# Threshold search of a graph stage: two staggered groups of tiles, the interval arithmetic and the scaling of x on GpSimd

## The reference, cut to what matters

```python
def _L1_xattn_ref(h, adj_raw, Wq, Wk, gamma_raw):
    ...
    sim = jnp.einsum('bhnd,bhmd->bnm', Q, K) / (jnp.sqrt(jnp.float32(d)) * H)
    k = max(1, int(n * TOP_K_RATIO))                      # 153 of 512
    topk_vals = jax.lax.top_k(sim, k)[0]
    threshold = topk_vals[:, :, -1:]
    sparse_mask = (sim >= threshold).astype(sim.dtype)
    A_learned = jax.nn.sigmoid(sim) * sparse_mask
    A_learned = (A_learned + jnp.swapaxes(A_learned, -1, -2)) * 0.5
    gamma = jax.nn.sigmoid(gamma_raw)
    return (1.0 - gamma) * adj_raw + gamma * A_learned
...
x = _layernorm(x + _L1_xattn_ref(ctx_512, x, ...), axis=-1)
```

## Time and profile before

| | us |
|---|---|
| median of 3 runs | 2637.19 |
| fastest and slowest of them | 2636.38, 2638.69 |
| the profiled execution | 2622.37 |
| its span, first to last instruction | 2620.70 |
| from the stage's first DMA issue to the next stage's first instruction | 1939.74 to 2129.29: 189.6 |
| the search, from DVE's first `mid` to the first mask | 1949.76 to 2066.28: 116.5 |
| masks and layer norm, to the next stage | 2066.28 to 2129.29: 63.0 |

### The profile page before, as it was taken

One profiled execution on the slowest core, in us unless ns is written; L12 is line 12 of the kernel. 1 busy time (PEld: TensorE's weight loads), 2 busy tenths in 40 slices (PEclk: granted clock), 3 DMA queues, 4 the chain that ended last, 5 costly groups with the idle time before them and its releaser, 6 DMA issues. The chain is left out here.

```text
span 2620.7 us, 32973 instructions
## 1 busy us (share of the span) xinstructions
PE 2007.4 (77%) x12156; PEld 1348.8 (51%) x12156; DVE 1763.1 (67%) x2779; ACT 1255.1 (48%) x2238; POOL 719.4 (27%) x662
## 2 busy tenths in 40 slices
PE   5999999377878787789986599999930159979990
PEld 4778777222222222355553477777720138857770
DVE  3456565366768675789997444656648867379986
ACT  2323232157656556367777232323228641169881
POOL 1111212200685950111210211121210002355535
PEclk8899999668889889899997689999965569989995
DMA  5332321356343420400000423232210030099976
GB/s 153 81 74 55 68 57 42 134 122 196 87 141 92 140 54 7 183 1 1 1 1 1 121 49 74 49 74 49 50 64 0 0 116 1 1 391 423 411 283 192
DMA packets 84584, 264.55 MB, mean 101 GB/s; under 512 B 17504, under 2 KB 19040, under 8 KB 73424
## 3 DMA queue, kind: packets, MB, share of 16 engines
q0 software_dynamic: 29632, 151.50, 17.3%
q1 hardware_dynamic: 53776, 110.75, 14.9%
q10 hardware_dynamic: 1024, 0.26, 0.0%
HBM read 169.87 MB, written 41.72 MB: 81 GB/s over the span
## 5 line engine op out<-in xcount | busy, mean ns | idle before, releaser
L880 DVE TENSOR_REDUCE x_negm<-x_M 128x2 f32<-128x1024 f32 x256 | 309.6, 1224 | 110.8 <-PE x_M L940 110.4
L829 ACT ACTIVATE x_PT<-x_T 128x512 f32<-128x512 f32 x512 | 280.2, 598 | 196.0 <-PE x_T L960 190.6
L322 ACT ACTIVATE L_attn_PT<-L_attn_T 128x512 f32<-128x512 f32 x320 | 175.3, 595 | 359.6 <-PE L_attn_T L524 359.6
L392 DVE TENSOR_REDUCE L_attn_negm<-L_attn_M 128x2 f32<-128x1024 f32 (+1 forms) x192 | 192.0, 1041 | 57.3 <-PE L_attn_M L505 56.9
L229 POOL DMA_DIRECT2D L_attn_QKS<-L_attn_HL x64 | 34.8, 544 | 597.3 <-ACT L_attn_HL L307 563.5
L960 PE MATMUL x_T<-x_QS,x_KS 49*128 49x512 f32 x512 | 139.4, 541 | 64.5 <-ACT x_PT L829 43.7
L522 PE MATMUL L_attn_T<-L_attn_QKS 97*128 97x256 f32 (+3 forms) x512 | 164.9, 384 | 10.0 <-DMA L_attn_QKS<-L_attn_mT 7.7
L969 PE MATMUL x_O<-x_PT,x_V 128*32 128x512 f32 x1024 | 155.7, 684 | 8.0 <-issue 8.0
L960 PEld LDWEIGHTS x_T<-x_QS,x_KS 49*128 49x128 f32 x512 | 51.5, 198 | 212.0 <-ACT x_PT L829 134.9
L940 PE MATMUL x_M<-x_KS,x_QS 48*128 48x512 f32 x512 | 119.1, 462 | 43.9 <-DMA x_QS<-x_xl 23.5
L503 PE MATMUL L_attn_M<-L_attn_QKS 96*128 96x384 f32 (+2 forms) x384 | 135.6, 422 | 19.2 <-DVE L_attn_XTL L366 11.5
(11 more groups left out here) (385 smaller groups left out, 5500.3 us busy)
## 6 DMA issues: line engine op xcount, KB each, us to landing
L_attn_QKS<-L_attn_HL SPq DMA_DIRECT2D x192, 128.0 KB, 4.7
L_attn_QKS<-L_attn_HL POOLq DMA_DIRECT2D x192, 128.0 KB, 4.1
moe_y_rows<-slots_YS SPq DMA_DIRECT2D x47, 256.0 KB, 7.0
x_WRAW<-in_w_gateT POOLq DMA_DIRECT2D x8, 1024.0 KB, 7.4
x_QS<-x_xh SPq DMA_DIRECT2D x128, 64.0 KB, 2.4
x_WRAW<-in_w_upT POOLq DMA_DIRECT2D x8, 1024.0 KB, 5.3
x_WRAW<-in_w_downT POOLq DMA_DIRECT2D x8, 1024.0 KB, 6.1
ffn_w<-x_WTER POOLq DMA_DIRECT2D x12, 512.0 KB, 3.0
```

The lines of the kernel that those rows point to most:

```text
L322: ac.activation(PT[:, s, bank], T[:, bank], ACT.Exp, scale=SCALE).then_inc(t_free, 1)
L392: last = ve.tensor_reduce(negm[:, g % 2, h0:h0 + nh, i], src, AX.X, ALU.max, negate=True)
L829: ac.activation(PT[:, s // 4, head(s), :], T[(STEPS_S * g + s) % 3][:], ACT.Exp, scale=SCALE).then_inc(t_free, 1)
L880: ve.tensor_reduce(negm[:, g % 2, u // 4:4:2, u % 4], m[:].rearrange("p (r k) -> p r k", r=2), AX.X, ALU.max, negate=True).then_inc(m_free, 1)
```

## The change

The search is written out (no hardware loop) and its tiles form two groups. Group 0 is tiles 0 to 3 (DVE) and 8 to 11 (ACT), group 1 is tiles 4 to 7 and 12 to 15; `side(col, g)` picks the eight columns of a group as 2 x 4. DVE and ACT count group 0, then group 1, then group 0 of the next halving, each when POOL has raised `mid_made` for it. POOL does the interval arithmetic of a group when both engines have counted it, in six steps of which each waits for the one before. After each halving POOL multiplies one tile of x by g2 in place; `XS` and ACT's 16 scalings are gone, and line 1626 (now 1635) reads x instead of `XS`. `graw` is loaded before the similarities, `gamma` is made before the search, and g2 and gh between DVE's first and second halving.

```diff
@@ block.sync @@
+            sp.dma_start(graw[:], A["gamma"]).then_inc(q["loaded"], 16)
             for b in (0, 2, 1, 3):
                 sp.dma_start(SIM[...], GR["sim"][b]).then_inc(sim_in[b], 16)
-            sp.dma_start(graw[:], A["gamma"]).then_inc(q["loaded"], 16)
+
+        @block.gpsimd
+        def _(pool):
+            PER = 6
+            for g in range(2):
+                gp.tensor_tensor(side(mid, g), side(low, g), side(width, g), ALU.add).then_inc(q["mid_made"], 1)
+            for n in range(HALVINGS):
+                for g in range(2):
+                    step = Steps(pool, q["halving"], 2 * n + g, PER)
+                    pool.wait_ge(q["counted_v"], 2 * n + g + 1)
+                    step(gp.tensor_scalar(side(take, g)[:, 0], side(count, g)[:, 0], TOPK - 0.5, None, ALU.is_ge))
+                    pool.wait_ge(q["counted_a"], 2 * n + g + 1)
+                    step(gp.tensor_scalar(side(take, g)[:, 1], side(count, g)[:, 1], S + 1.5 - 2 * TOPK, None, ALU.is_le))
+                    step(gp.tensor_tensor(side(take, g), side(take, g), side(width, g), ALU.mult))
+                    step(gp.tensor_tensor(side(low, g), side(low, g), side(take, g), ALU.add))
+                    step(gp.tensor_scalar(side(width, g), side(width, g), 0.5, None, ALU.mult))
+                    step(gp.tensor_tensor(side(mid, g), side(low, g), side(width, g), ALU.add))
+                    pool.sem_inc(q["mid_made"], 1)
+                if n == 0:
+                    pool.wait_ge(q["gam2"], 2)
+                gp.tensor_scalar(XF[:, n, :], XF[:, n, :], g2[:, 0:1], 1.0, ALU.mult, ALU.mult).then_inc(q["scaled"], 1)
@@ block.scalar @@
+            act.wait_ge(q["loaded"], 16)
+            ac.activation(gamma[:], graw[:], ACT.Sigmoid).then_inc(q["gam"], 1)
             for b in range(DVE_TILES // NT, NB):
                 act.wait_ge(sim_in[b], 16)
-            with act.Fori(0, HALVINGS) as n:
-                act.wait_ge(q["mid_done"], n + 1)
-                for t in range(DVE_TILES, NTILE):
-
-                    inst = ac.activation(seen_a[:, t - DVE_TILES, :], SIM[:, t, :], ACT.Sign, scale=-1.0,
-                                         bias=mid[:, t:t + 1], accum_out=count[:, t:t + 1])
-                inst.then_inc(q["counted_a"], 1)
-            act.wait_ge(q["loaded"], 16)
-            ac.activation(gamma[:], graw[:], ACT.Sigmoid).then_inc(q["gam"], 1)
+            for n in range(HALVINGS):
+                for h in range(2):
+                    act.wait_ge(q["mid_made"], 2 * n + h + 1)
+                    for t in range(DVE_TILES + HALF * h, DVE_TILES + HALF * (h + 1)):
+                        inst = ac.activation(...)
+                    inst.then_inc(q["counted_a"], 1)
...
-            act.wait_ge(q["gam2"], 2)
...
-                if b:
-                    act.wait_ge(q["z_done"], b * NT)
-                for i in range(NT):
-                    ac.activation(XS[:, i, :], XF[:, b * NT + i, :], ACT.Identity, scale=g2[:, 0:1]).then_inc(q["xs"], 1)
@@ block.vector @@
-            with dve.Fori(0, HALVINGS) as n:
-                k = Steps(dve, q["halved"], n, 4)
-                ve.tensor_tensor(mid[:], low[:], width[:], ALU.add).then_inc(q["mid_done"], 1)
-                dve.wait_ge(q["mid_done"], n + 1)
-                for t in range(DVE_TILES):
...
-                k(ve.scalar_tensor_tensor(out=take[:, 0:DVE_TILES], ...))
-                dve.wait_ge(q["counted_a"], n + 1)
-                k(ve.scalar_tensor_tensor(out=take[:, DVE_TILES:], ...))
-                k(ve.tensor_tensor(low[:], low[:], take[:], ALU.add))
-                k(ve.tensor_scalar(width[:], width[:], 0.5, None, ALU.mult))
+            for n in range(HALVINGS):
+                for h in range(2):
+                    dve.wait_ge(q["mid_made"], 2 * n + h + 1)
+                    for t in range(HALF * h, HALF * (h + 1)):
+                        inst = ve.tensor_scalar(...)
+                    inst.then_inc(q["counted_v"], 1)
+                if n == 0:
+                    dve.wait_ge(q["gam"], 1)
+                    pre = Steps(dve, q["gam2"], 0, 2)
...
+            dve.wait_ge(q["mid_made"], 2 * HALVINGS + 2)
...
-                        dve.wait_ge(q["xs"], b * NT + i + 1)
+                        dve.wait_ge(q["scaled"], b * NT + i + 1)
                         ve.scalar_tensor_tensor(out=XF[:, b * NT + i, :], in0=SUM[:, i, :], scalar=gh[:, 0:1],
-                                                in1=XS[:, i, :], op0=ALU.mult, op1=ALU.add).then_inc(q["z_done"], 1)
+                                                in1=XF[:, b * NT + i, :], op0=ALU.mult, op1=ALU.add).then_inc(q["z_done"], 1)
```

More of the change, by code:

```diff
@@ L1495, in stage_graph @@
         SUM = sb("SUM", [P, NT, S], F32)
-        XS = sb("XS", [P, NT, S], F32)
         seen_v = sb("seen_v", [P, DVE_TILES, S], BF16)
         seen_a = sb("seen_a", [P, NTILE - DVE_TILES, S], BF16)
+        HALF = DVE_TILES // 2
+        side = lambda col, g: col[:].rearrange("p (e t) -> p e t", e=2)[:, :, HALF * g:HALF * (g + 1)]
         graw, gamma, g2, gh = (small(n, 1) for n in ("graw", "gamma", "g2", "gh"))
@@ L1505, in stage_graph @@
         PP = [ps(f"P{i}", 2 * BANK) for i in range(4)]
-        names = ("loaded mid_done counted_v counted_a gam gam2 "
-                 "sigm xs masked turned summed halved z_done stat norm shifted applied between")
+        names = ("loaded mid_made counted_v counted_a halving scaled gam gam2 "
+                 "sigm masked turned summed z_done stat norm shifted applied between")
         sim_in = [sem(f"sim_in{b}") for b in range(NB)]
@@ L1533, in _ @@
         def _(act):
+            act.wait_ge(q["loaded"], 16)
+            ac.activation(gamma[:], graw[:], ACT.Sigmoid).then_inc(q["gam"], 1)
             for b in range(DVE_TILES // NT, NB):
                 act.wait_ge(sim_in[b], 16)
-            with act.Fori(0, HALVINGS) as n:
-                act.wait_ge(q["mid_done"], n + 1)
-                for t in range(DVE_TILES, NTILE):
-                    inst = ac.activation(seen_a[:, t - DVE_TILES, :], SIM[:, t, :], ACT.Sign, scale=-1.0,
-                                         bias=mid[:, t:t + 1], accum_out=count[:, t:t + 1])
-                inst.then_inc(q["counted_a"], 1)
-            act.wait_ge(q["loaded"], 16)
-            ac.activation(gamma[:], graw[:], ACT.Sigmoid).then_inc(q["gam"], 1)
+            for n in range(HALVINGS):
+                for h in range(2):
+                    act.wait_ge(q["mid_made"], 2 * n + h + 1)
+                    for t in range(DVE_TILES + HALF * h, DVE_TILES + HALF * (h + 1)):
+                        inst = ac.activation(seen_a[:, t - DVE_TILES, :], SIM[:, t, :], ACT.Sign, scale=-1.0,
+                                             bias=mid[:, t:t + 1], accum_out=count[:, t:t + 1])
+                    inst.then_inc(q["counted_a"], 1)
             for b in range(DVE_TILES // NT):
                 act.wait_ge(sim_in[b], 16)
-            act.wait_ge(q["gam2"], 2)
             def norm_tile(t):
@@ L1591, in _ @@
-            dve.wait_ge(q["gam"], 1)
-            pre = Steps(dve, q["gam2"], 0, 2)
-            pre(ve.tensor_scalar(g2[:], gamma[:], -1.0, 2.0, ALU.mult, ALU.add))
-            pre(ve.tensor_scalar(gh[:], gamma[:], 0.5, None, ALU.mult))
+            for n in range(HALVINGS):
+                for h in range(2):
+                    dve.wait_ge(q["mid_made"], 2 * n + h + 1)
+                    for t in range(HALF * h, HALF * (h + 1)):
+                        inst = ve.tensor_scalar(seen_v[:, t, :], SIM[:, t, :], mid[:, t:t + 1], 0.0, ALU.is_ge, ALU.add,
+                                                accum_out=count[:, t:t + 1])
+                    inst.then_inc(q["counted_v"], 1)
+                if n == 0:
+                    dve.wait_ge(q["gam"], 1)
+                    pre = Steps(dve, q["gam2"], 0, 2)
+                    pre(ve.tensor_scalar(g2[:], gamma[:], -1.0, 2.0, ALU.mult, ALU.add))
+                    pre(ve.tensor_scalar(gh[:], gamma[:], 0.5, None, ALU.mult))
```

10 lines of the change are left out of this document (removed).

## The result

| | median us | runs | lowest to highest |
|---|---|---|---|
| kernel before, measured beside it | 2639.44 | 9 | 2636.38 to 2650.58 |
| changed kernel | 2626.00 | 9 | 2612.05 to 2635.34 |

What follows compares the result with a forecast made beforehand. The bound was taken to be ACT's counting with DVE's small arithmetic bare behind it in each search halving. Terms summed to -20.3 us, from 2637.2 to 2616.9 us; the range was 2614.5 to 2626.0.

Steps and rivals of the forecast that it cites:

- This chain is the bound: Search: ACT's eight counts, then DVE's small arithmetic lying bare for 1.29 us, make the halving's period of 7.04 us.
- counting, with the borders: Search: ACT's counts take 90.6 instead of 111.30 us, -20.7; 31 new group borders on ACT add 0.6.
- end of the search: From ACT's last count to the first mask: 2.77 us before, POOL's chain of 1.77 after, -1.0.
- last scaling against the first masks: POOL's sixteenth scaling beside DVE's first mask: each can hold the other up, 0 to 0.69 us, taken as +0.3.
- start: Start of the graph stage: SP issues `graw` ahead of the similarities, shifting everything by +0.5 us (0 to 0.6).
- XS gone: Masks: 16 activations of 0.71 us leave ACT, which waited for DVE there; gain 0.
- rival C: Search: group borders on ACT cost 0.21 us each, +5.9, kernel at 2622.8 us; chance 0.07.
- B: POOL's scaling is a slow form, 2.07 us, making POOL the bound; kernel at 2623.1 us; chance 0.22.
- D: Search: POOL is stretched by DVE's counting, 0.8 us more than ACT per halving; kernel at 2628.9 us; chance 0.07.
- E: Search: each POOL step waits for a whole DVE count, 47.4 us over the forecast, 2664.3; chance 0.05.
- It lay 14.8 below the median of the runs, so I carry the difference over: Whole kernel: the profiled execution's 2602.1 us after the change is raised to a median of 2616.9.
- F: Outside the search: something gives the gain back, so no gain; chance 0.04.

Runs made afterwards that it cites:

- a_nostag: Changed kernel without the stagger: both groups wait for the second `mid`; ratio to the kernel before 1.0019, graph stage 194.2 us.
- a_xs: Changed kernel with the scaling of x back on ACT in the masks, none on POOL; ratio to the kernel before 0.9898, graph stage 167.7 us.
- a_slow: Changed kernel with POOL's scaling written as subtract 0, then multiply by g2; ratio to the kernel before 0.9963, graph stage 172.2 us.

## Why the prediction was right, and where it was off

**The bound and the cover: right.** "This chain is the bound" and "ACT never waits for a `mid`" held in every halving; `a_nostag` shows that without the cover nothing of the gain is left. Term by term:

| term | predicted | measured |
|---|---|---|
| counting, with the borders | -20.7 + 0.6 | -20.96 |
| end of the search | -1.0 | -1.13 |
| last scaling against the first masks | +0.3 | +0.29 over the masks |
| start | +0.5 | +0.45 |
| XS gone | 0 | none found (`a_xs`) |
| graph stage | -20.3 | -21.35 |

The borders are the one term that was too high: I took 0.02 us each, and the pitch across all 128 counts, 0.705, is a little under the 0.707 read from a single halving. So they cost nothing that shows, and rival C falls. POOL's chain from the last accumulator read to the mask was 1.64 us, 1.77 in the prediction; its load for a halving 3.82 + 0.77 = 4.59 us, 4.65 in the prediction.

**B: the mechanism is real, this form isn't the slow one.** The step that was uncertain was multiply-and-multiply, in no row of before; it takes 0.69. I had gone by its operands. The time came out right and the reason didn't: `a_slow` has the same operands, in the other order, and takes 2.01, while the two pointers of the earlier trace rows take 2.07. That multiply-and-multiply is on the fast side was luck. What the three slow forms on record share is the subtraction as their first operation; whether it is that, or in `a_slow` the order of pointer and constant, no run here separates.

**D and E: refuted.** 32 chains in the search have steps of 0.20 to 0.24 us beside DVE's counts. The stretch of the earlier trace rows stood beside the plain `tensor_scalar` of the normalisation; no run varied that one. The one collision of the search's end is that of the masks with POOL's last scaling, 3.17 and 1.19 us, and it grows with the number of scalings. The Trainium skill (SBUF — State Buffer, Who interferes with whom) sorts them so: forms that write out an accumulator don't take the shared port, instructions with two SBUF inputs collide with a GpSimd one that reads. Here the traces agree: the counts, of the first kind, left POOL's steps at 0.20 to 0.24, and the masks, of the second, collided. That one engine holds the port pair for a whole instruction, as the prediction has it from the same section, is not what the masks show: beside the scaling of 2.01 us in `a_slow` all four of them lost 0.43 us together, with most of their time inside its 2.50. The Trainium skill (GPSIMD Engine Reference, Engine selection) has two-input work at about twice VectorE's time; here it was 0.20 against 0.17 us on these small tiles. `a_nostag` lost time, in the page's direction, but by a chain of five steps where DVE had four behind ACT's last count, so it doesn't test the factor.

**The level: wrong.** The step that failed is "It lay 14.8 below the median of the runs, so I carry the difference over", with "1 us of scatter; three runs lay within 2.3". The three runs said little of how executions spread: nine of the kernel before reach from 2636.38 to 2650.58, 17 of a later session from 2616.15 to 2643.77. In traces the spread sits mostly in two places that this change doesn't touch: the cross-attention stage, 481 to 493 us from its first write of `x_Z` to its last norm, which is most of why the graph stage starts between 1937.0 and 1950.6, and the routing stage, 164 to 183. The forecast median was low by 9.1 us while the gain in the stage was 1.1 us better than forecast. Of the 9.1, 2.3 are the level of the kernel before (median 2639.44 now, 2637.19 then); the other 6.9 are a drop of 13.4 us between the medians where 20.3 was forecast and the stage gave 21.35. That the two stages took it in those runs too is likely from the one pair of traces, not shown. The ratio of the first comparison, times 2637.2, gives 2621.1, and the later pairs gave 0.9903 and 0.9926, some 25 and 20 us. The stage alone would be 21.35 / 2639.4 = 0.8%, a ratio of 0.9919: inside the two later intervals, just under the first (0.9921). The range held the time, but by B's place in it, not because B happened.

**F, which had no row,** is what the first pair of traces seemed to show: a gain given back in a stage behind. It took both kernels in the same session to see that the giving back was none.

What stays open: what makes TensorE's matmuls of the routing stage come 1.4 us apart for 12 to 19 us in some sessions and not in others, and what moves the cross-attention stage by up to 11 us. No run here tells it.

## What to carry to other kernels

Where two engines count and a short serial step between rounds lies bare, split the data into two groups and stagger them: the step then costs nothing as long as it fits under one group's counting (here 1.6 to 1.8 us under 2.8) and the whole load of the engine that does it fits under a round (4.6 us under 5.6; at 5.9, in `a_slow`, it was the bound). That engine may be a slower one. Moving the step without the stagger lost time. Compare traces by stage before a gain is said to be lost, and run the unchanged kernel beside the changed one: 19 us of "loss" in a stage behind belonged to neither.

## What the runs showed of the hardware

- TensorE can lose its pace without any releaser in the profile: share_UG's matmuls up to 1.42 us apart instead of 0.23, in a stretch of some 20 us. The first gap is at 2222.5; the granted clock fell from 2.4 to 1.2 GHz only near 2232, so the lower clock follows the stall and stays for some 5 us behind it. The stall came with the session (0, 12 or 17 to 19 us), whichever kernel ran.
- GpSimd's two-operation instruction on 128 x 512 f32 takes 0.69 us as multiply by pointer, then by constant, and 2.01 as subtract constant, then multiply by pointer.
- GpSimd beside VectorE: steps of 0.20 to 0.24 us undisturbed by counts with accumulators; against two-input masks both sides lose, 0.50 and 0.43 us for one scaling. Two scalings cost the masks 0.87, and one of 2.01 us costs them no more than one of 0.69.
- Four loads of 1 MB issued together by one queue become usable one by one: the first 5.0 us after their issue began, then one every 2.5 us. Waiting for each alone brought ACT's first count 7.6 us forward, of which 3.8 were kept.
